# Attention layer of 16 graphs on one core: two transposed copies of x by the batch's parity, and TensorE's V stretch written twice

## What is computed

```
qkv  = (x @ w_qkv)                      # per head: q, k, v of 1024 x 64
attn = softmax(where(adj == 0, -inf, (q @ k.T) * hd ** -0.5))
o    = (attn @ v) @ w_proj + b_proj
ln   = (o - mean(o)) * rsqrt(var(o) + 1e-5) * gamma + beta
out  = layernorm(x + o + ln)
```

## Time and profile before

| | |
|---|---|
| median of 3 runs | 3217.51 us (3217.07 to 3221.09) |
| profiled execution | 3214.41 us |
| its span on the core | 3212.6 us |
| TensorE matmuls busy | 3035.8 us, 94% |
| ScalarE busy | 2621.1 us, 82% |
| GpSimd busy | 2500.2 us, 78% |
| VectorE busy | 2481.6 us, 77% |
| DMA | 648.05 MB, 202 GB/s |

### The profile page before, as it was taken

The page is one execution under the profiler, slowest core; times in us unless marked ns, Lnnn a source line. Parts: engine busy times, 40 slices in busy tenths (PEclk is TensorE's granted clock), DMA queues, the critical chain, the costliest instruction groups (busy, mean ns, idle before and its releaser), DMA issues.

```text
span 3212.6 us, 121377 instructions
## 1 busy us (share of the span) xinstructions
PE 3035.8 (94%) x42504; PEld 1892.9 (59%) x42504; DVE 2481.6 (77%) x4601; ACT 2621.1 (82%) x3849; POOL 2500.2 (78%) x1543
## 2 busy tenths in 40 slices
PE   6989999999999999999999999999999999999984
PEld 3656656656665656656566666656656566665552
DVE  5567777878778787787878878787787877878775
ACT  5888888888888888888888888888888888888871
POOL 2777878787887878888787887878878788887883
PEclk9999999999999999999999999999999999999997
DMA  7999999999999999999999999999999999999993
GB/s 208 192 190 199 208 198 211 199 211 205 206 212 197 214 202 206 213 199 211 200 210 205 207 211 197 215 201 206 214 199 208 199 210 206 207 212 187 202 197 97
DMA packets 2187078, 648.05 MB, mean 202 GB/s; under 512 B 2135408, under 2 KB 2135408, under 8 KB 2186992
## 3 DMA queue, kind: packets, MB, share of 16 engines
q1 hardware_dynamic: 2133808, 548.28, 93.1%
q10 hardware_dynamic: 53184, 98.59, 9.3%
HBM read 76.28 MB, written 33.55 MB: 34 GB/s over the span
## 4 chain that ended last, share of the span: by engine, by line
POOL 45%; issue 31%; PE 10%; SPq 7%; DMA 2%; DVE 2%; ACT 1%; POOLq 1%; DVEq 0%; ACTq 0%
POOL p_split L780 37%; SPq L309 7%; POOL x_res L796 4%; PE scores_a L411 3%; PE side L375 2%; DMA pt<-p_split 2%; POOL norm L804 2%; POOL norm L799 2%; PE side L357 2%; PE proj L392 1%; PE pv_bank L432 1%; PE pv_bank L434 1%; PE pv_bank L433 1%; POOL shift L807 1%; POOLq L779 1%
## 5 line engine op out<-in xcount | busy, mean ns | idle before, releaser
L780 POOL TENSOR_TENSOR p_split<-p,p_split 128x1024 f16<-128x1024 f32 x1024 | 2178.6, 2144 | 642.8 <-ACT p_split L517 641.1
L504 ACT ACTIVATE p<-p,row_min 128x1024 f32<-128x1024 f32 x1024 | 1170.7, 1144 | 279.0 <-DVE row_min L662 277.1
L517 ACT ACTIVATE p_split<-p 128x1024 f16<-128x1024 f32 x1024 | 1047.2, 1046 | 120.4 <-DMA pt<-p_split 119.9
L432 PE MATMUL pv_bank<-v_both,pt 128*128 128x64 f16 x8192 | 830.5, 193 | 39.2 <-DMA pt<-p_split 31.2
L662 DVE CUSTOM_DVE_ANT_0 p<-scores_a,mask_q 128x1024 f32<-128x1024 f32 x512 | 626.2, 1223 | 309.4 <-PE scores_b L411 259.9
L434 PE MATMUL pv_bank<-v_both,pt 128*128 128x64 f16 x8192 | 831.4, 194 | 0.0
L433 PE MATMUL pv_bank<-v_both,pt 128*128 128x64 f16 x8192 | 831.3, 194 | 0.0
L432 PEld LDWEIGHTS pv_bank<-v_both,pt 128*128 128x128 f16 x8192 | 741.0, 98 | 126.5 <-issue 62.1
L433 PEld LDWEIGHTS pv_bank<-v_both,pt 128*128 128x128 f16 x8192 | 730.6, 98 | 67.9 <-issue 1.6
L434 PEld LDWEIGHTS pv_bank<-v_both,pt 128*128 128x128 f16 x8192 | 731.4, 98 | 0.0
L375 PE MATMUL side<-xt,w_hi 128*128 128x512 f16 x2048 | 636.0, 382 | 7.8 <-DVE q_lo L641 7.2
(11 more groups left out here) (80 smaller groups left out, 4411.2 us busy)
## 6 DMA issues: line engine op xcount, KB each, us to landing
x_in<-in_x ACTq DMA_DIRECT2D x60, 512.0 KB, 5.3
x_res<-in_x ACTq DMA_DIRECT2D x120, 256.0 KB, 3.5
out<-x_res ACTq DMA_DIRECT2D x120, 256.0 KB, 3.3
pt<-p_split SPq DMA_TRANSPOSE x1024, 4.9
pt<-in_adj SPq DMA_DIRECT2D x8, 512.0 KB, 10.0
ot<-in_L_gnn_w_qkv SPq DMA_DIRECT2D x4, 768.0 KB, 9.7
p<-in_x SPq DMA_DIRECT2D x8, 256.0 KB, 5.0
p<-in_x ACTq DMA_DIRECT2D x8, 256.0 KB, 8.5
```

The source lines that it names most:

```text
L432: nc.tensor.matmul(o, hi, v_hi, start=(kt == 0 and at == 0), stop=False, skip_group_check=True)
L504: nc.scalar.activation(p32[:, slot, :], p32[:, slot, :], ACT.Exp, bias=row_min[:, slot:slot + 1], scale=-1.0, accum_out=row_sum[:, head:he ...
L517: nc.scalar.activation(p_split[:, head % RING, HI, :], p32[:, head % RING, :], ACT.Copy).then_inc(hi_done, 1)
L780: nc.gpsimd.tensor_tensor(p_split[:, slot, LO, :], p32[:, slot, :], p_split[:, slot, HI, :], ALU.subtract).then_inc(lo_done, 1)
```

## The change

`xt` becomes two whole copies of 8 tiles, and batch b uses copy b & 1. X0 and X1 write the next batch's tiles straight into the other copy. `place`, `waiting`, `at_end`, `copy_tile`, `COPY` and the semaphores `x_copied` are gone. Q and K read the copy whose number is computed from g. For V the copy's number must be known where the weights are loaded, so in the loop TensorE's slots with V items (`V_SLOTS`, 4 to 11) stand twice in the program, once for each copy, each behind an `If` on the batch's parity, and with them the scores and the products with v of units 1 and 2 that lie in these slots. `ORDER`, `COST` and some slots of takes and norms are other numbers.

```diff
-ORDER = [("Q1", 0, 12), ("X0", 0, 4), ("V0", 0, 48), ("V1", 0, 48), ("P0", 0, 3), ("O1", 0, 4), ("P0", 3, 7),
+ORDER = [("Q1", 0, 12), ("X0", 0, 4), ("V0", 0, 48), ("V1", 0, 48), ("P0", 0, 4), ("O1", 0, 4), ("P0", 4, 7),
...
-COST = {"Q": 8, "V": 2.5, "O": 4, "K": 10, "P": 9, "X": 8}
+COST = {"Q": 9, "V": 2.5, "O": 4, "K": 10, "P": 9, "X": 5}
...
+V_SLOTS = [s for s in range(SLOTS) if any(kind[0] == "V" for kind, i in ITEMS[s])]
...
-TAKE_DVE = {"Q1": 4, "X0": 5, "V0": 12, "V1": 12, "O1": 14, "X1": 18, "Q0": 22, "K0": 29, "K1": 30, "O0": 30}
-
-COPY = [12, 13, 13, 15, 16, 17, 17]
-LOAD_X = 20
+TAKE_DVE = {"Q1": 4, "X0": 5, "V0": 10, "V1": 11, "O1": 14, "X1": 15, "Q0": 22, "K0": 29, "K1": 30, "O0": 30}
+LOAD_X = 18
...
-              {"stats": 30, "aggr": 31, "eps": 33, "add": 34, "power": 35, "scale": 36, "sum": 38, "stats2": 38,
+              {"stats": 30, "aggr": 31, "eps": 33, "add": 34, "power": 35, "scale": 34, "sum": 38, "stats2": 38,
...
-        xt = sb("xt", [P, 2 * T - 1, 2, KC, P], F16)
+        xt = sb("xt", [P, 2, T, 2, KC, P], F16)
...
-            def side_matmul(g, kind, i):
+            def side_matmul(g, kind, i, side_of_x):
...
-                    mm = nc.tensor.matmul(bank[:, c * P:(c + 1) * P], xt[:, place(t), rows, k, :],
+                    mm = nc.tensor.matmul(bank[:, c * P:(c + 1) * P], xt[:, side_of_x, t, rows, k, :],
...
-                    if i == 0 and kind == "K1" and active(g, "X1"):
+                    if i == 0 and kind == NEXT_FIRST and active(g, "X1"):
                         wait_alone(pe, side_dve, side_done(g, "X1"))
-                    if i == 0 and kind == NEXT_FIRST:
-                        wait_alone(pe, x_copied[0], batch(g + 1))
-                    if i == 0 and kind == "K1":
-                        wait_alone(pe, x_copied[1], batch(g + 1))
...
-                                          xt[:, place(4 * half):place(4 * half) + 4, x_half, k, :],
+                                          xt[:, parity(batch(of)), 4 * half:4 * half + 4, x_half, k, :],
...
+            def stretch(g, slots, side_of_x):
+                for s in slots:
+                    u, j = s // QUARTERS, s % QUARTERS
+                    if j == 0 and active(g, "A"):
+                        unit_scores(g, u)
+                    if j % 2:
+                        times_v(g, u, j // 2)
+                    for kind, i in ITEMS[s]:
+                        side_matmul(g, kind, i, side_of_x)
+
             def body(g):
-                for u in range(UNITS):
-                    if active(g, "A"):
-                        unit_scores(g, u)
-                    for j in range(QUARTERS):
-                        if j % 2:
-                            times_v(g, u, j // 2)
-                        for kind, i in ITEMS[u * QUARTERS + j]:
-                            side_matmul(g, kind, i)
+
+                if known(g):
+                    stretch(g, range(SLOTS), parity(batch(g)))
+                    return
+                stretch(g, range(0, V_SLOTS[0]), None)
+                for side_of_x in range(2):
+                    with pe.If((batch(g) & 1) == side_of_x):
+                        stretch(g, range(V_SLOTS[0], V_SLOTS[-1] + 1), side_of_x)
+                stretch(g, range(V_SLOTS[-1] + 1, SLOTS), None)
...
-                    nc.scalar.activation(xt[:, waiting(g, half), HI, :, :],
+                    nc.scalar.activation(xt[:, parity(batch(g + PAIRS)), pair(g) * 2 + half, HI, :, :],
...
-                wait_alone(dve, side_act, side_done(g, kind))
+                wait(dve, side_act, side_done(g, kind))
...
-            def copy_tile(g, t):
-
-                if t == 0:
-                    wait_alone(dve, side_ready, side_done(g, "V1"))
-                    wait_alone(dve, side_dve, side_done(g, "X0"))
-                move = nc.vector.tensor_copy(xt[:, place(t), :, :, :].rearrange("p h k n -> p (h k n)"),
-                                             xt[:, waiting(t // 2, t % 2), :, :, :].rearrange("p h k n -> p (h k n)"))
-                if t in (3, 6):
-                    move.then_inc(x_copied[t // 4], 1)
...
-                    for t in range(7):
-                        if COPY[t] == s:
-                            at_end(dve, g, lambda: copy_tile(g, t))
```

More of the change, by code:

```diff
@@ L214, in attention_block @@
         x_first_turned, x_first_hi, x_first_lo = sem("x_first_turned"), sem("x_first_hi"), sem("x_first_lo")
-        x_copied = sems("x_copied", 2)
         x_res_loaded, stored = sems("x_res_loaded", 2), sems("stored", 2)
@@ L236, in bodies @@
                 body(g)
[L238 to L251, removed]
         def heads(g, u, ab):
@@ L470, in first_high @@
                 act.wait_ge(x_first_turned, t + 1)
-                nc.scalar.activation(xt[:, place(t), HI, :, :], side[t % 2][:, :].rearrange("p (k n) -> p k n", k=KC), ACT.Copy
+                nc.scalar.activation(xt[:, 0, t, HI, :, :], side[t % 2][:, :].rearrange("p (k n) -> p k n", k=KC), ACT.Copy
                                      ).then_inc(x_first_hi, 1)
@@ L595, in first_low @@
                 dve.wait_ge(x_first_hi, t + 1)
-                nc.vector.tensor_tensor(xt[:, place(t), LO, :, :], side[t % 2][:, :].rearrange("p (k n) -> p k n", k=KC),
-                                        xt[:, place(t), HI, :, :], ALU.subtract).then_inc(x_first_lo, 1)
+                nc.vector.tensor_tensor(xt[:, 0, t, LO, :, :], side[t % 2][:, :].rearrange("p (k n) -> p k n", k=KC),
+                                        xt[:, 0, t, HI, :, :], ALU.subtract).then_inc(x_first_lo, 1)
             def prepare_mask(t):
@@ L630, in take @@
                 elif kind[0] == "X":
-                    tile = waiting(g, half)
-                    nc.vector.tensor_tensor(xt[:, tile, LO, :, :], bank[:, :].rearrange("p (k n) -> p k n", k=KC),
-                                            xt[:, tile, HI, :, :], ALU.subtract).then_inc(side_dve, 1)
+                    at, tile = parity(batch(g + PAIRS)), pair(g) * 2 + half
+                    nc.vector.tensor_tensor(xt[:, at, tile, LO, :, :], bank[:, :].rearrange("p (k n) -> p k n", k=KC),
+                                            xt[:, at, tile, HI, :, :], ALU.subtract).then_inc(side_dve, 1)
                 elif kind[0] == "V":
```

## The result

The changed kernel takes 3835.57 us (median of 4 runs, 3829.12 to 3839.01) against 3217.29 us for the kernel before: 1.192 times its time, 95% interval 1.190 to 1.194. That is far above the forecast of 3345 us and above its range. The sign, the place and the number of the new waits were as forecast; what each costs was not.

The account below looks back on a forecast made before the run. TensorE was taken to bound a plain group, copies the batch's end. From 3214.4 us, minus 74 for copies, plus 11 for branches and register instructions, plus 193 for code waits gave 3344, kept as 3345 us; range 3235 to 3440.

Parts of the forecast that it names:

- The sign: Whole kernel: slower at chance 0.83, same 0.04, faster 0.13.
- The bound and the copies: TensorE bounds a plain group; removing copies at 15 batch ends gains 74 us, bounds 65 to 78.
- The loop's code: TensorE's longer pass outgrows its code store: two waits at back edge and V jump, 107 in all, 193 us.
- The rival with one wait per pass: TensorE's loop: block's place goes by its number, jump finds its target, 53 waits cost 106 us; 3257 us, chance 0.30.
- The rival with the store large enough: TensorE's loop: store holds the new pass or hides the waits, queue 8 stays silent; 3151 us, chance 0.13.
- The price of a wait: Each TensorE code wait in the loop: 1.8 us, from 1.0 to 3.5; all on the path.
- the toll: Loop passes: packets among transposes add 27 us, dearer code waits 268 us, clock may halve; 3446 us, chance 0.10.
- The moved items: Q1, X0 transposes, P0 and Q0 change slots in each group; costed at nothing, given ScalarE's and VectorE's room.
- The load's slot: Load of x_in issued at slot 18 instead of 20; costed at nothing.
- Branches and register instructions: TensorE's extra address instructions and two branches per pass: 0.2 us in each of 54 passes, 11 us, bounds 0 and 54.

Follow-up runs that it names:

- the kernel with nine blocks: Kernel before with 201 never-executed instructions and a branch added in TensorE's loop, blocks 25 to 33 with the one fetched ahead: 3632.50 us, ratio 1.130.
- the kernel without copies: Kernel before without the seven copies at a batch's end, their conditions and TensorE's waits for them; x partly stale: 3138.26 us, ratio 0.9759.
- both with four places: Changed kernel, only V's matmuls twice, in four places of two slots, loop shifted to fit: new order 3204.65 us, slots of the kernel before 3170.94 us.
- The version with two places and the old order: Changed kernel, only V's matmuls twice, in two places of four slots, loop shifted to fit, order and slots of the kernel before: 3156.83 us, ratio 0.9817.

## Why the prediction was wrong

**The bound and the copies: right.** TensorE was the bound of a plain group and the copies were the batch's end. Forecast 74 us, measured 78, at the upper edge of my 65 to 78 us.

**The loop's code: right in kind and number.** Two waits per pass, 107 in all, at the two places named, and ten packets per pass: 591 = 59 + 532, which is 53 x 10 and two more. Of the two forms of store, the one with two waits held. The rival with one wait per pass (3257 us) had the wrong store: the kernel with nine blocks fetched nine per pass, not two. The rival with the store large enough (3151 us) fell at once with 591 packets. The Trainium skill (Advanced Engine Details and Errata, ISA Cache) with its 128 KB in lines of 16 KB on TensorE, eight lines, was right to the line: eight blocks fit and nine do not. The "Only 2 cache lines!" of the same section does not hold for TensorE here. The Trainium skill also says (Runtime: NRT & Kernel Launch, Instruction fetch mechanics) that a taken branch to code outside the window, which it calls one of two pages, waits for a DMA; that wait is now seen, at 4.1 to 6.1 us in the median, with a window of eight blocks.

**The price of a wait: the step that failed.** I put it at 1.8 us, between 1.0 and 3.5. TensorE's idle time is 492.5 / 107 = 4.6 us, above my upper end. I had taken a DMA's time from issue to landing as the whole: 2.0 us of a 256 KB store for the value, 3.5 us of a 256 KB load for the upper bound. A branch to missing code took 4.1 us in the median at its best place, 3.6 at the shortest, and of these 4.1 the packet itself is only 0.9; my lower bound had that size right, and 3.2 us stand before and behind it. The wait was the one term with no row of its own, and all of the result hung on it; a bound from rows of another kind of transfer was no bound. With every term at its worst bound (65 us gained, 54 for branches, 374 for waits) my sum gives 3577 us, already far above the 3440 us at which I closed the range, and still far below the 3836 us measured.

**The clock: left out of the sum.** Against the kernel without copies (span 3139.7 us, TensorE busy 3008.0) the changed kernel's span is 697.5 us longer. Of these 492.5 are the waits, and 3214.3 - 3008.0 = 206.3 us are matmuls that took longer, which together are the whole. The granted clock fell from 0.990 to 0.926 over the span. By the clock record of the two traces matmuls ran at 1.2 GHz for 451 and 32 us; half of the difference, 210 us, is the 206. I had the half-speed stretch at the batch's end before me and mentioned the toll only in a rival, at 0.10; the changed trace has 112 stretches at 1.2 GHz, the one without copies nine.

By the measured terms my sum would read 3214.4 - 78 + 492.5 + 206.3 = 3835 us. This is bookkeeping, not a test: both new terms are differences to the kernel without copies, and what branches and moved items cost in the changed kernel is inside them.

**The moved items: the term was mis-sized.** I said that they cost nothing because ScalarE and VectorE have room. They cost 34 us in a loop that fits. TensorE's own order is part of it: before Q0 it waits for no engine 25.6 us in 54 waits in the new order, 0.47 us each, and 13.9 us in the old (both with four places); a wait of 10.9 us in 54 before a product with v comes on top, and the matmuls are busy for 15 us more. That address instructions are late there because little is queued ahead is my reading; no run moves them alone. The load's slot, which I also put at nothing, is free in a loop that fits and costs 171 us where code packets stream.

**Branches and register instructions.** 11 us was forecast, with bounds of 0 and 54. The version with two places and the old order costs 18.6 us over the kernel without copies, so the size was right within the bounds, for a kernel with four conditional branches per pass where the changed one has two.

## What to carry to other kernels

Before a stretch of a loop is duplicated, count the instructions of one pass on TensorE, weight loads included, and the blocks that the pass touches from where it begins: TensorE here holds eight blocks of 256 with the one fetched ahead, and the ninth cost 13% of the kernel's time. When a pass is just too long, shorten the duplicated part to what differs or move the loop's beginning, which costs nothing. And when a wait has no row in the trace, do not close its range with the time of another kind of transfer; ask also what the clock does after it.

## What was not expected of the hardware

- Eighty more instructions ahead of a loop made the kernel 418 us faster (3632.50 to 3214.04 us), and a hundred fewer dead ones inside it did the same (3213.91 us).
- A branch to missing code takes 4.1 us (median) where one packet starts in the wait and 5.7 to 6.1 us where two do, and in the kernel with 201 dead instructions a wait costs 7.8 us of time: 324.2 us in 53 waits are 6.1 us each, and the rest is mostly the half clock behind it (TensorE's busy time grew by 100 us).
- Writing the loop out is not free for a kernel whose transposes fill the DMA engines (share about 1.0): with 344 packets on queue 8 instead of 59 a transpose takes 5.6 to 5.7 us to land, not 4.9, and the written-out kernels lost 92 us (old order) and more.
- With such a stream, moving one 512 KB load by two slots changed its landing from 4.7 to 11.6 us and the kernel by 171 us. Why it then lands so late was not tried further.
